# Expert stages of a two-layer kernel: new rings for rows, placements and outputs, and another order of TensorE's and ScalarE's work

## The reference

```
x = x + attention0(layernorm(x), ctx)        # 8 heads of 64
x = x + experts0(layernorm(x)) + shared(...) # 16 experts, the best 2 per token, inner width 64
x = x + attention1(layernorm(x), ctx)        # 16 heads of 16, masked, its own layer norm
x = x + experts1(layernorm(x))               # 32 experts, the best 4 per token, inner width 128
```

## Time and profile before

| what | value |
|---|---|
| time, median of 3 runs | 1792.15 us (1791.57 to 1800.09) |
| time of the profiled execution | span 1784.9 us, the runs beside it 1792.15 us in the median |
| busy, of the span | PE 86%, DVE 75%, ACT 60%, POOL 61% |
| experts of layer 0 | 925.00 to 1075.40 us, 150.40 us |
| experts of layer 1 | 1436.50 to 1718.20 us, 281.70 us |

### The profile page before, as it was taken

The page is one execution under the profiler, slowest core; times in us unless marked ns, Lnnn a source line. Parts: engine busy times, 40 slices in busy tenths (PEclk is TensorE's granted clock), DMA queues, the critical chain, the costliest instruction groups (busy, mean ns, idle before and its releaser), DMA issues.

```text
span 1784.9 us, 43889 instructions
## 1 busy us (share of the span) xinstructions
PE 1540.2 (86%) x14968; PEld 1241.0 (70%) x14968; DVE 1333.0 (75%) x2901; ACT 1071.7 (60%) x3276; POOL 1093.7 (61%) x1111
## 2 busy tenths in 40 slices
PE   4999999999999999989977773998895179999966
PEld 3888888888888888866646661565563169898955
DVE  3899889999998899976624443698887248787876
ACT  3888888888888888844324432665651045555510
POOL 2766767667667676646735565547776736566642
PEclk9999999999999999989989886999996579999989
DMA  6500000000000000022244435102222945454447
GB/s 181 175 19 20 19 20 11 20 20 20 19 19 20 19 20 19 8 84 79 85 144 142 147 108 188 48 29 97 79 74 99 324 142 161 154 162 151 154 188 285
DMA packets 103080, 167.65 MB, mean 94 GB/s; under 512 B 20223, under 2 KB 75980, under 8 KB 102480
## 3 DMA queue, kind: packets, MB, share of 16 engines
q1 hardware_dynamic: 77136, 105.37, 19.0%
q0 software_dynamic: 22272, 56.15, 8.6%
q10 hardware_dynamic: 3456, 3.34, 0.6%
HBM read 95.31 MB, written 75.76 MB: 96 GB/s over the span
## 4 chain that ended last, share of the span: by engine, by line
PE 66%; issue 11%; DVE 9%; POOL 5%; another core or an unknown queue 2%; DMA 2%; SPq 1%; ACT 1%; ACTq 0%; DVEq 0%; POOLq 0%
PE layers_banks L323 14%; PE layers_banks L297 13%; PE layers_banks L309 9%; PE layers_banks L877 7%; PE layers_banks L888 4%; PE layers_banks L1250 3%; PE layers_banks L282 3%; PE layers_banks L286 3%; PE layers_banks L865 2%; POOL l_by_token L991 2%; PE layers_banks L1263 1%; DVE weights L1843 1%; PE layers_banks L2128 1%; PE layers_banks L1610 1%
## 5 line engine op out<-in xcount | busy, mean ns | idle before, releaser
L461 POOL TENSOR_TENSOR w_down<-w_down,layers_arena 128x1024 f32<-128x1024 f32 x256 | 483.5, 1893 | 234.9 <-DVE layers_arena L420 234.0
L387 ACT ACTIVATE w_down<-layers_banks,layers_arena 128x256 f32<-128x256 f32 x1024 | 468.7, 498 | 1.8 <-DVE layers_arena L414 1.8
L991 POOL DMA_INDIRECT l_by_token<-layers_arena x240 | 245.7, 1024 | 194.2 <-issue 100.7
L425 DVE COPY w_down<-layers_banks 128x1024 f32<-128x1024 f32 x256 | 312.0, 1219 | 40.6 <-PE layers_banks L309 37.1
L414 DVE TENSOR_REDUCE layers_arena<-layers_banks 128x4 f32<-128x1024 f32 x256 | 309.4, 1209 | 41.0 <-PE layers_banks L297 40.6
L297 PE MATMUL layers_banks<-layers_arena 64*128 64x256 f32 x2048 | 279.7, 385 | 2.9 <-ACT w_down L387 2.2
L323 PE MATMUL layers_banks<-w_down,layers_arena 128*64 128x256 f32 x2048 | 250.6, 386 | 1.6 <-DVE w_down L425 1.3
L387 ACT ACTIVATION_READ_ACCUMULATOR w_down<-layers_banks,layers_arena 128x1 f32 x1024 | 237.9, 232 | 0.0
L877 PE MATMUL layers_banks<-layers_arena 128*128 128x128 f32 x1600 | 207.9, 283 | 25.1 <-ACT layers_arena L915 18.0
L1160 POOL DMA_INDIRECT l_rows_in<-layers_arena,l_routing_group_slots x192 | 189.7, 988 | 57.7 <-issue 44.9
L309 PEld LDWEIGHTS layers_banks<-ident,w_down 64*128 64x128 f32 x4096 | 168.7, 138 | 78.0 <-issue 72.0
(11 more groups left out here) (225 smaller groups left out, 2508.4 us busy)
## 6 DMA issues: line engine op xcount, KB each, us to landing
layers_arena<-l_rows_in SPq DMA_DIRECT2D x240, 136.0 KB
weights<-l_by_token SPq DMA_DIRECT2D x32, 512.0 KB, 9.7
layers_arena<-in_ctx SPq DMA_DIRECT2D x64, 128.0 KB, 2.8
layers_arena<-l_by_token SPq DMA_DIRECT2D x32, 256.0 KB, 2.7
weights<-in_w_gu SPq DMA_DIRECT2D x16, 512.0 KB
l_rows_in<-zeros SPq DMA_DIRECT2D x1, 4352.0 KB
x_sb<-in_x SPq DMA_DIRECT2D x32, 128.0 KB
w_down<-in_w_down SPq DMA_DIRECT2D x1, 4096.0 KB
```

The source lines that it names most:

```text
L387: last = nc.scalar.activation(prob[:, n % 4, c, :], ps_s[:, n % 2, c, :], ACT.Exp, bias=negmax[:, n % 2, c:c + 1], accum_out=sums[:, n % 2 ...
L425: nc.vector.tensor_copy(prob_t[:, n // 2 % 2, n % 2, :, :, :].rearrange("p k c (d s) -> p d (k c) s", d=2), ps_t[:, :, :, :].rearrange("p ...
L461: nc.gpsimd.tensor_tensor(prob[:, n % 4, :, :], prob[:, n % 4, :, :], rsum[:, n % 2, :].unsqueeze(2).to_broadcast([P, 4, A_N]), ALU.mult). ...
L991: pool.indirect_dma_start(m.by_token, bass.IndirectOffsetOnAxis(ap=place, axis=0), outs[:, r % RING, b, :], None, bounds_check=T * m.K - 1 ...
```

## The change

The ring of `rows` has 6 pairs in place of 8. Two small rings of 16 pairs, `dest` and `weight`, hold the places and weights of the rows: ACT copies them out of the row buffer (two tiny instructions per pair) behind its copy of the transposed rows, and counts `tails_kept`. DVE reads the weight and POOL the place from these rings. So SP's load of pair r waits only for `tails_kept` of pair r - 6. The ring `outs` and its semaphores are 8 deep in place of 4; the weighing waits for the store of pair n - 8, and also for `tails_kept` of its own pair.

In PE's step the order becomes gate and up of pair r + 1, transposes of pair r + 2, down of pair r - 1. In ACT's step the weight copies come first; then, in layer 0, the Silu of pair r + 1 and behind it the copy of the transposed rows of pair r + 2 with the tails; in layer 1, the copy with the tails and behind it the sigmoid of pair r + 1.

```diff
-    BODY, RING = 8, 4
+    BODY, RING, OUTS, TAILS = 6, 4, 8, 16
...
-    outs = ph.sbuf("outs", [P, RING, 2, H])
+    outs = ph.sbuf("outs", [P, OUTS, 2, H])
+    dest = ph.sbuf("dest", [P, TAILS, 2])
+    weight = ph.sbuf("weight", [P, TAILS, 2])
...
             if r >= BODY:
-                done(sp, x_made, 0, r - BODY)
-                sp.wait_ge(rows_stored[r % RING], 32 * ((r - BODY) // RING + 1))
+                sp.wait_ge(tails_kept, r - BODY + 1)
...
         def step(it, r):
+            if exists(it, r + 1):
+                gate_up(it, r + 1)
             if exists(it, r + 2):
                 transposes(it, r + 2)
-            if exists(it, r + 1):
-                gate_up(it, r + 1)
             if exists(it, r - 1):
                 down(it, r - 1)
...
+        def transposed(q):
+            done(act, x_made, 0, q)
+            done(act, gu_made, 0, q - 2)
+            nc.scalar.activation(rows_t[:, q % 2, :, :, :], ps_x[:, q % 2, :, :, :], ACT.Copy).then_inc(x_ready, 1)
+            if q >= TAILS:
+                act.wait_ge(rows_stored[q % OUTS], 32 * ((q - TAILS) // OUTS + 1))
+            nc.scalar.activation(dest[:, q % TAILS, :].bitcast(I32),
+                                 rows[:, q % BODY, :, DEST].bitcast(I32), ACT.Copy)
+            nc.scalar.activation(weight[:, q % TAILS, :], rows[:, q % BODY, :, WEIGHT], ACT.Copy).then_inc(tails_kept, 1)
...
         def step(it, r):
             if exists(it, r + 2):
+                weights_of(r + 2)
+            if bias is None and exists(it, r + 1):
+                function(r + 1)
             if exists(it, r + 2):
+                transposed(r + 2)
+            if bias is not None and exists(it, r + 1):
+                function(r + 1)
...
         def weigh(n):
             done(dve, y_made, 0, n)
-            if n >= RING:
-                dve.wait_ge(rows_stored[n % RING], 32 * (n // RING))
+            dve.wait_ge(tails_kept, n + 1)
+            if n >= OUTS:
+                dve.wait_ge(rows_stored[n % OUTS], 32 * (n // OUTS))
             for b in range(2):
-                last = nc.vector.tensor_scalar(outs[:, n % RING, b, :], ps_y[:, n % 2, b, 0:H],
-                                               rows[:, n % BODY, b, WEIGHT:WEIGHT + 1], None, ALU.mult)
+                last = nc.vector.tensor_scalar(outs[:, n % OUTS, b, :], ps_y[:, n % 2, b, 0:H],
+                                               weight[:, n % TAILS, b:b + 1], None, ALU.mult)
...
-                place = rows[:, r % BODY, b, DEST:DEST + 1].bitcast(I32)
+                place = dest[:, r % TAILS, b:b + 1].bitcast(I32)
```

More of the change, by code:

```diff
@@ L794, in experts @@
     rows_loaded = [ph.sem(f"rows_loaded{n}") for n in range(BODY)]
-    rows_stored = [ph.sem(f"rows_stored{n}") for n in range(RING)]
+    rows_stored = [ph.sem(f"rows_stored{n}") for n in range(OUTS)]
+    tails_kept = ph.sem("tails_kept")
     x_made, x_ready, w_ready = ph.sem("x_made"), ph.sem("x_ready"), ph.sem("w_ready")
@@ new lines, in weights_of, with function @@
+        def weights_of(q):
+            e = experts_of(0, q)
+            done(act, gu_made, 0, q - 2)
+            for b in range(2):
+                last = nc.scalar.activation(w_now[:, q % 2, b, :, :].rearrange("p k n -> p (k n)"),
+                                            w_gu[:, bass.ds(e[b], 1), :, :].rearrange("p a k n -> p (a k n)"), ACT.Copy)
+            last.then_inc(w_ready, 1)
+        def function(q):
+            done(act, a_ready, 0, q - 2)
+            if bias is None:
+                done(act, gu_made, 0, q)
+                nc.scalar.activation(glu[I:P, q % 2, :, :], ps_gu[0:I, q % 2, 0, :, :], ACT.Silu).then_inc(function_ready, 1)
+            else:
+                done(act, gate_ready, 0, q)
+                nc.scalar.activation(glu[:, q % 2, :, :], gate[:, q % 2, :, :], ACT.Sigmoid, scale=ALPHA)\
+                    .then_inc(function_ready, 1)
@@ L989, in store @@
             for b in range(2):
-                place = rows[:, r % BODY, b, DEST:DEST + 1].bitcast(I32)
+                place = dest[:, r % TAILS, b:b + 1].bitcast(I32)
                 pool.indirect_dma_start(m.by_token, bass.IndirectOffsetOnAxis(ap=place, axis=0),
-                                        outs[:, r % RING, b, :], None, bounds_check=T * m.K - 1, oob_is_err=False)\
-                    .then_inc(rows_stored[r % RING], 16)
+                                        outs[:, r % OUTS, b, :], None, bounds_check=T * m.K - 1, oob_is_err=False)\
+                    .then_inc(rows_stored[r % OUTS], 16)
         for r in range(NP):
@@ L997, in all_stored @@
     def all_stored(eng):
-        for n in range(RING):
-            eng.wait_ge(rows_stored[n], 32 * (NP // RING))
+        for n in range(OUTS):
+            eng.wait_ge(rows_stored[n], 32 * (NP // OUTS))
     return all_stored
```

## The result

The changed kernel is slower: 1802.1 us in the median of 10 runs (1791.9 to 1811.9) against 1794.7 (1788.8 to 1800.1) for the kernel before, ratio 1.0044 (95% interval 1.0024 to 1.0064), some 8 us. A second set of 12 runs (changed_again) gave 1.0044 again (1.0024 to 1.0065). The forecast was 1789 us, 3.4 us less than before, and no measurable change. The time lies within the stated range of 1766 to 1812, but it moved the other way.

A forecast was written before the change was run, and what follows sets the result against it. Layer 0 was taken as bound by POOL's scatters and its pauses, layer 1 by DVE's loop. Loads -1 and two starts of -1.2, all else 0, gave -3.4 from 1792.15: 1789 us, range 1766 to 1812.

The forecast's parts named there:

- Pauses and rings: Layer 0: POOL's 3-us pauses remain; outputs eight deep are worth 0, bounds 0 and -32.0 us.
- That the tails cost nothing: Both expert stages: ACT's two tiny copies, 0.42 us a pair, are hidden by ACT's idle time: 0.
- PE's order ... still under 3.30: 0: Layer 1: the new order makes PE's loop 3.12 us for 3.09, still hidden under 3.30 a pair: 0.
- the cover of 3.30: Layer 1: DVE's loop, 3.30 us a pair, hides PE's longer loop; without that cover 2.4 us.
- 2.23 for the loop: Layer 0: PE's loop becomes 2.20 + 0.03 us a pair, under POOL's 2.58: 0.
- ACT's order: Start of each expert stage: weight copies ahead of the row copy let the first gate and up come earlier, -1.2 us each.
- the starts at -1.2 each: Starts of layers 0 and 1: weights copied while ACT idles for the rows, -1.2 us in each layer.
- The slower rival: Both layers: transposes' end known late, ACT's row copy delays PE's gate and up; one layer 1806 us, both 1823; chance 0.29.

The follow-up runs named there:

- rings_alone: Changed kernel with PE's and ACT's old order put back, leaving only rings, deeper outputs and tail copies; ratio to before 0.9996 (0.9973 to 1.0018).
- orders_no_scatter: Changed kernel with POOL's scatters left out, SP storing outputs to consecutive rows (output not the reference's); 1748.5 us, 0.9772 of before.
- start_old_order: Changed kernel with PE's old order in the first five steps of each expert stage only; ratio to before 1.0049 (1.0032 to 1.0065).
- rings_act_order_2: Changed kernel with only PE's order put back, run once more for a second profile; one run, 1785.8 us beside 1788.2.
- longer_lead: Changed kernel with transposes and ACT's copy one pair further ahead (r + 3, third slot in rows_t); ratio to before 1.0078 (1.0056 to 1.0100).
- rings_act_order: Changed kernel with only PE's order put back, ACT's new order kept; first set of runs, ratio to before 1.0087 (1.0058 to 1.0116).
- lead_and_rest: longer_lead with POOL resting behind every second pair of layer 0; ratio to before 1.0042 (1.0015 to 1.0069).

## Why the prediction was wrong

*Pauses and rings: right.* POOL's later wait for the weighing is 32.0 us in both profiles, and rings_alone is at 0.9996 of before. By the estimate of 2.3 us for a transfer, worked out from the fit in the Trainium skill, "DMA: Bandwidth & Descriptors", section "Anatomy of one DMA — SWDGE (gpsimd) path", a deeper ring was worth nothing here; rings_alone agrees, though no run shows a scatter landing. That the tails cost nothing was right too: the two of a pair take 196 and 194 ns on average.

*"PE's order ... still under 3.30: 0": this step failed.* Its place was right and its size was off. In layer 1 the loop came out at 3.24, not 3.12: the way from gate and up to the next transposes is 1.86 where I took 1.79 from gate and up to down, the end of the copy to gate and up 0.14 where I took 0.10, and 0.01 more lies between transposes and copy. And the cover of 3.30 was a mean that holds stalls; the median step was 3.21. That is 80 x 0.03 = 2.4 us; orders_no_scatter shows the full price, 12.7 us, when DVE's late clip no longer hides it. The prediction had named this as what would make it wrong: a loop through PE's signals that the new order lengthens in every pair.

In layer 0 I took 2.23 for the loop; with PE at its higher level the shortest step that keeps coming back is 2.37 in the changed kernel, for 2.20 before. That is still under POOL's 2.58, but at the lower level a pair took 3.68 (the start), and I set no price on that. Behind the start, five of the six profiles with PE's old order in layer 0 and no rests show 130.8 to 133.1 us and one 139.1, in the mean 133.3; the six with the new order and a lead of two (start_old_order from its sixth step on) 134.5 to 144.3, in the mean 139.0. Compared chip by chip (in the mean where a chip has two), the new order's is the longer each time, by 1.5 to 10 us. My reading is that the chain counts between two pauses, where PE has to make as many pairs as it can; no run shows that by itself. The granted clock goes along with it: between the first scatter and the last gate and up of layer 0 it was at its lower level for 9 to 27 us in the six profiles with the old order (18 in the mean, 27 in the one of 139.1) and for 10 to 41 in the six with the new (26), and over the twelve the stretch tends to be longer where that time is longer (correlation 0.82). Which of the two brings the other was not tested.

With 3.1 us at the start (12.4 and 15.4 in the mean) and 2.9 in layer 1 (276.2 and 279.1) the profiles differ by 11.6 us, where the runs show 8 (4 to 12). Part of that is the choice of executions: in the mean those profiled with the old order were 6 us faster than the medians of their sets (rings_act_order_2 has none), those with the new 1 us slower.

*"ACT's order", the starts at -1.2 each: this step failed too, with its sign.* The weights did come before the rows, and gate and up of layer 0 began 1.87 us behind the first transposes (3.06 before). But from the second pair on each pair hung on transposes, copy and gate and up in a row, at half PE's later speed, and the granted clock rose 6 us later than before; the sum had no term for either. The first scatter came 2.9 us later; in layer 1 it came 0.5 later, which is within what the other profiles spread (14.7 to 18.0 us).

*The slower rival had the right place, ACT's copy on PE's path, and the wrong cause.* It asked for a late end of the transposes in layer 1 and a pair above 3.3 us; there the copy starts 0.04 us behind them and the pair takes 3.24, and in layer 0 POOL's pauses over 2 us did not become more (10 for 11). The chain is long enough without any lateness.

*What stays open.* How much is PE's order and how much ACT's is not shown: the profiles point to PE's, and longer_lead mends layer 0 with ACT's order in place, but one set of rings_act_order lost 0.87%. Whether the clock or the chain makes layer 0 longer behind its start is not shown either. That a faster PE makes POOL wait more in layer 1 was seen twice (longer_lead, lead_and_rest) and not explained; the granted clock was at its lower level for 36 and 40 us of layer 1 there, for 10 in the changed kernel.

## What to carry to other kernels

A copy between two steps of TensorE needs other work of TensorE as its cover. Moving the two steps next to each other makes a loop whose length is the sum of both and the copy, and it should be set against the median step of the stage, not against the mean with its stalls. Where an engine pauses while everybody waits for everybody, look for one signal that two independent waiters share, and test it by giving the suspected engine a rest. A start without earlier pairs to fill the gaps has to be followed instruction by instruction, at the clock that it will be granted.

## What the runs showed of the hardware

While POOL issues indirect scatters back to back (0.98 us each, 0.30 apart), DVE and ACT take up results of TensorE up to 4.5 us behind their modelled end, in layer 0 of the kernel before 1.0 to 1.3 us behind the end of POOL's last scatter in all 11 pairs that are over 1 us late, in 6 of them DVE and ACT's Silu within 0.1 us of each other. With a rest of about 1.5 us behind every pair the weighing starts 0.04 us behind its down in 34 of 40 pairs, and without scatters in all of them. Which path is shared was not found. Since the ends of PE's instructions are modelled, the profiles can't tell a late end from a late signal. The Trainium skill, "SBUF — State Buffer", section "Who interferes with whom", says that PE and ACT never wait on anyone at SBUF's ports; no run here tests that, and the cause can't be read from that table.

The start of layer 0 is one stretch whose length goes with TensorE's granted clock: 15.2 to 15.6 us to the first scatter where the clock rose 12.9 to 14.1 us behind the first transposes, and 12.1 to 13.0 where it rose after 3.4 to 7.0. In the changed kernel PE was idle 0.78 us in each of the pairs of 3.68 us before it rose.
